# Two attention score products written as full-height matmuls over zero-padded keys, in place of pairs of half-height ones, in a two-layer decoder kernel

## The reference, cut to what matters

```python
# self-attention, 16 heads of 64
q = jnp.einsum('bsm,hmd->bhsd', x, kernel[0])
k = jnp.einsum('bsm,hmd->bhsd', x, kernel[1])
scores = jnp.einsum('bhsd,bhtd->bhst', q, k) * scale
attn = jax.nn.softmax(scores, axis=-1)
out = jnp.einsum('bhst,bhtd->bhsd', attn, v)
...
# cross-attention, 16 heads of 16, keys and values from the context
q = _split_heads(query @ Wq.T + bq)
k = _split_heads(key @ Wk.T + bk)
scores = jnp.einsum('bhnd,bhmd->bhnm', q, k)
attn = jax.nn.softmax(scores, axis=-1)
```

## Time and profile before

| | |
|---|---|
| median of the runs | 1388.13 us |
| the profiled execution, its own time | 1388.13 us |
| its span (first to last instruction) | 1386.4 us |
| mean granted TensorE clock | 0.963 of full |
| busy: TensorE / VectorE / ScalarE / GpSimd | 1161.0 / 750.3 / 732.8 / 380.4 us |
| chain that ended last | TensorE 64%, VectorE 15%, ScalarE 10% |

### The profile page before, as it was taken

How to read it: one execution, slowest core, us unless ns; L and a number is a source line. 1 busy time by engine, 2 the same in 40 slices (tenths; PEclk the granted TensorE clock), 3 DMA queues, 4 the chain that set the end, 5 groups by cost and what they waited for, 6 DMA issues and landing times.

```text
span 1386.4 us, 19831 instructions
## 1 busy us (share of the span) xinstructions
PE 1161.0 (84%) x6458; PEld 770.1 (56%) x6458; DVE 750.3 (54%) x1815; ACT 732.8 (53%) x1866; POOL 380.4 (27%) x881
## 2 busy tenths in 40 slices
PE   6897876999899976799889977699989997779955
PEld 2454544775555644676455554477555564467643
DVE  1563375655464368546545437655545436855644
ACT  1555345575465355557456534556645635555833
POOL 1232301542034310153213430154203332016420
PEclk9998998999999999899999999899999999989978
DMA  9101300000000000000000000000000000000000
GB/s 248 63 1 54 93 1 1 1 1 1 1 0 17 1 23 1 3 0 1 1 1 16 1 23 1 2 1 1 1 1 0 17 1 1 1 1 1 1 0 16
DMA packets 27895, 20.77 MB, mean 15 GB/s; under 512 B 14412, under 2 KB 27148, under 8 KB 27660
## 3 DMA queue, kind: packets, MB, share of 16 engines
q1 hardware_dynamic: 27196, 17.83, 5.0%
q10 hardware_dynamic: 592, 1.59, 0.3%
HBM read 17.32 MB, written 2.10 MB: 14 GB/s over the span
## 4 chain that ended last, share of the span: by engine, by line
PE 64%; DVE 15%; ACT 10%; issue 7%; POOL 3%; DMA 1%; ACTq 0%; SPq 0%; POOLq 0%; DVEq 0%
PE PS L495 8%; PE PS L559 7%; PE PS L841 7%; PE PS L482 5%; PE PS L572 5%; PE PS L547 4%; PE PS L586 4%; PE PS L617 4%; PE PS L602 4%; PE PS L815 3%; PE PS L706 2%; PE PS L692 2%; PE PS L853 2%; ACT work L1316 1%; DVE work L1591 1%
## 5 line engine op out<-in xcount | busy, mean ns | idle before, releaser
L1849 POOL TENSOR_TENSOR rstd<-var,minus_half 128x2 f32<-128x2 f32 x80 | 56.4, 705 | 522.3 <-DVE nmean L1409 522.3
L1138 ACT ACTIVATE work<-PS,nmax 128x256 f32<-128x256 f32 x256 | 117.9, 472 | 99.5 <-DVE nmax L1461 99.5
L1844 POOL TENSOR_TENSOR pool_pause<-minus_half 128x1 f32<-128x1 f32 x96 | 18.6, 194 | 440.3 <-DVE inv L1468 359.0
L1316 ACT ACTIVATE work<-PS,nmax 120x256 f32<-120x256 f32 x256 | 118.4, 483 | 24.7 <-DVE nmax L1726 24.5
L841 PE MATMUL PS<-work 128*120 128x256 f32 x512 | 119.7, 384 | 3.9 <-ACT work L1101 3.9
L1461 DVE TENSOR_REDUCE nmax<-PS 128x2 f32<-128x512 f32 x128 | 82.2, 684 | 68.7 <-PE PS L572 68.2
L1863 POOL TENSOR_SCALAR work<-work,inv 128x256 f32<-128x256 f32 x256 | 118.1, 483 | 0.0
L1726 DVE TENSOR_REDUCE nmax<-PS 120x2 f32<-120x512 f32 x128 | 86.3, 686 | 53.3 <-PE PS L841 48.6
L841 PEld LDWEIGHTS PS<-work 128*120 128x120 f32 x512 | 90.8, 183 | 29.8 <-issue 12.8
L1903 POOL TENSOR_SCALAR work<-work,head_mask 128x120 f32<-128x120 f32 x256 | 107.3, 447 | 0.0
L1109 ACT ACTIVATE x_room<-res,nshift,rstd 128x256 f32<-128x256 f32 x96 | 52.3, 592 | 101.9 <-POOL nshift L1851 101.9
(11 more groups left out here) (258 smaller groups left out, 2439.9 us busy)
## 6 DMA issues: line engine op xcount, KB each, us to landing
xa<-in_x_dram SPq DMA_DIRECT2D x4, 512.0 KB, 3.7
out_dram<-x_room SPq DMA_DIRECT2D x4, 512.0 KB, 3.7
rows<-in_rows_dram ACTq DMA_DIRECT2D x1, 1536.0 KB, 8.5
late<-in_L_attn_W_dram SPq DMA_DIRECT2D x2, 768.0 KB, 7.6
wv<-in_L_attn_kernel_dram SPq DMA_DIRECT2D x2, 512.0 KB, 8.9
wq<-in_L_attn_kernel_dram SPq DMA_DIRECT2D x2, 512.0 KB, 9.5
wk<-in_L_attn_kernel_dram SPq DMA_DIRECT2D x2, 512.0 KB, 7.7
wo<-in_L_attn_WO_dram SPq DMA_DIRECT2D x2, 512.0 KB, 7.7
```

The source lines that it names most:

```text
L1138: op = act.activation(e0[:, u % 2, st, hh, :], bank(2 + hh)[:, st * S:(st + 1) * S], ACT.Exp, bias=nmax0[:, u % 2, hh, st:st + 1], accum_o ...
L1316: op = act.activation(e1[:, par, r, kv, :], bank(4 + n % 4)[0:M, kv * S:(kv + 1) * S], ACT.Exp, bias=nmax1[:, par, r, kv:kv + 1], accum_ou ...
```

## The change

Keys of the self-attention are kept in a tile twice as wide, `k0[P, 2, NB, 2, S]`. It is zeroed once at the start; for each group VectorE copies head 0's 64 partitions into the columns of head 0 and head 1's 64 partitions into the columns of head 1, in two copies, so that each column holds one head's key and zeros for the other head. `scores0` then makes one product with all 128 rows and 512 columns for each query block `st`: two products instead of four. Banks now belong to query blocks, no longer to heads, and the waits between `scores0`, `max0` and `exp0` go by query block. In the cross-attention GpSimd masks 8 copies of the keys for each group instead of 4 (with `head_mask` instead of `quarter_mask`, which goes), and `scores_x` makes its two products of 480 columns with 128 rows instead of 64.

```diff
-        quarter_mask = sb("quarter_mask", [P, HC // 2])
-        k0 = sb("k0", [P, 2, NB, S])
+        k0 = sb("k0", [P, 2, NB, 2, S])
-        kxm = view(work, 6144, P, [2, HC // 2, M])
+        kxm = view(work, 6144, P, [2, HC, M])
...
         def scores0(it, u):
-                if u > 0:
-                    pe.wait_ge(p0_done.sem, p0_done.at(it, 2 * u))
                 for st in range(TS):
-                    for hh in range(2):
-                        rows = slice(hh * DH0, (hh + 1) * DH0)
-                        mm = pe.matmul(bank(2 + hh)[:, st * S:(st + 1) * S],
-                                       q0[rows, j % 2, b * S + st * P:b * S + (st + 1) * P],
-                                       k0[rows, j % 2, b, :], start=True, stop=True)
-                        if st == TS - 1:
-                            mm.then_inc(s0_done.sem, 1)
+                    if u > 0:
+                        pe.wait_ge(p0_done.sem, p0_done.at(it, TS * (u - 1) + st + 1))
+                    pe.matmul(bank(2 + st), q0[:, j % 2, b * S + st * P:b * S + (st + 1) * P],
+                              k0[:, j % 2, b, :, :], start=True, stop=True).then_inc(s0_done.sem, 1)
...
         def scores_x(it, n):
                 for g in range(2):
-                    rows = slice(64 * g, 64 * (g + 1))
-                    mm = pe.matmul(bank(4 + 2 * (n % 2) + g)[:, 0:4 * M], qx[rows, c, b * S + st * P:b * S + (st + 1) * P],
-                                   kxm[rows, n // 2 % 2, :, :], start=True, stop=True)
+                    mm = pe.matmul(bank(4 + 2 * (n % 2) + g)[:, 0:4 * M], qx[:, c, b * S + st * P:b * S + (st + 1) * P],
+                                   kxm[:, n // 2 % 2, 4 * g:4 * g + 4, :], start=True, stop=True)
...
         def exp0(it, u):
-                for hh in range(2):
-                    act.wait_ge(m0_done.sem, m0_done.at(it, 2 * u + hh + 1))
+                for st in range(TS):
+                    act.wait_ge(m0_done.sem, m0_done.at(it, TS * u + st + 1))
...
-                    for st in range(TS):
-                        op = act.activation(e0[:, u % 2, st, hh, :], bank(2 + hh)[:, st * S:(st + 1) * S], ACT.Exp,
+                    for hh in range(2):
+                        op = act.activation(e0[:, u % 2, st, hh, :], bank(2 + st)[:, hh * S:(hh + 1) * S], ACT.Exp,
...
         def keep_k0(it, j):
-                dve.tensor_copy(k0[:, j % 2, :, :].rearrange("p b s -> p (b s)"), bank(1)).then_inc(k0_kept.sem, 1)
+                for hh in range(2):
+                    rows = slice(hh * DH0, (hh + 1) * DH0)
+                    op = dve.tensor_copy(k0[rows, j % 2, :, hh, :], bank(1)[rows, :].rearrange("p (b s) -> p b s", b=NB))
+                op.then_inc(k0_kept.sem, 1)
...
+            dve.memset(k0[:, :, :, :, :], 0.0)
             dve.memset(vxp[:, :, :, :, :], 0.0)
...
                 def mask_x(m):
-                    for h in range(HC // 2):
+                    for h in range(HC):
                         op = pool.tensor_scalar(kxm[:, m % 2, h, :], kx[:, c, b * M:(b + 1) * M],
-                                                quarter_mask[:, h:h + 1], 1.0, ALU.mult, ALU.mult)
+                                                head_mask[:, h:h + 1], 1.0, ALU.mult, ALU.mult)
```

More of the change, by code:

```diff
@@ L183, in decoder @@
         q0 = view(work, 12288, P, [2, N])
-        k0 = sb("k0", [P, 2, NB, S])
+        k0 = sb("k0", [P, 2, NB, 2, S])
         e0 = view(work, 4096, P, [2, TS, 2, S])
         e0t = view(work, 6144, P, [2, 2, TS, S])
-        nmax0 = sb("nmax0", [P, 2, 2, TS])
-        sum0 = sb("sum0", [P, 2, 2, TS])
-        inv0 = sb("inv0", [P, 2, 2, TS])
+        nmax0 = sb("nmax0", [P, 2, TS, 2])
+        sum0 = sb("sum0", [P, 2, TS, 2])
+        inv0 = sb("inv0", [P, 2, TS, 2])
         o0t = view(work, 8192, P, [J, N])
@@ L324, in decoder @@
         U0 = J * NB
-        s0_done, m0_done, p0_done = signal("s0_done", U0 * 2), signal("m0_done", U0 * 2), signal("p0_done", U0 * 2)
+        s0_done, m0_done, p0_done = signal("s0_done", U0 * TS), signal("m0_done", U0 * TS), signal("p0_done", U0 * TS)
         i0_done, n0_done = signal("i0_done", U0), signal("n0_done", U0)
@@ L392, in decoder @@
         gsum_done, gg2_wide, base_done = signal_rounds("gg_dve_steps", ("sum", "layer 2 in columns", "base"))
-        N_CONST = 12
+        N_CONST = 11
         N_ZEROED = 1
@@ L1132, in exp0 @@
             def exp0(it, u):
-                for hh in range(2):
-                    act.wait_ge(m0_done.sem, m0_done.at(it, 2 * u + hh + 1))
+                for st in range(TS):
+                    act.wait_ge(m0_done.sem, m0_done.at(it, TS * u + st + 1))
                     if u > 1:
                         act.wait_ge(t0_done.sem, t0_done.at(it, 2 * (u - 1)))
-                    for st in range(TS):
-                        op = act.activation(e0[:, u % 2, st, hh, :], bank(2 + hh)[:, st * S:(st + 1) * S], ACT.Exp,
-                                            bias=nmax0[:, u % 2, hh, st:st + 1], accum_out=sum0[:, u % 2, hh, st:st + 1])
+                    for hh in range(2):
+                        op = act.activation(e0[:, u % 2, st, hh, :], bank(2 + st)[:, hh * S:(hh + 1) * S], ACT.Exp,
+                                            bias=nmax0[:, u % 2, st, hh:hh + 1], accum_out=sum0[:, u % 2, st, hh:hh + 1])
                     op.then_inc(p0_done.sem, 1)
@@ L1455, in keep_k0 @@
                 dve.wait_ge(k0_done.sem, k0_done.at(it, j + 1))
-                dve.tensor_copy(k0[:, j % 2, :, :].rearrange("p b s -> p (b s)"), bank(1)).then_inc(k0_kept.sem, 1)
+                for hh in range(2):
+                    rows = slice(hh * DH0, (hh + 1) * DH0)
+                    op = dve.tensor_copy(k0[rows, j % 2, :, hh, :], bank(1)[rows, :].rearrange("p (b s) -> p b s", b=NB))
+                op.then_inc(k0_kept.sem, 1)
             def max0(it, u):
-                for hh in range(2):
-                    dve.wait_ge(s0_done.sem, s0_done.at(it, 2 * u + hh + 1))
-                    dve.tensor_reduce(nmax0[:, u % 2, hh, :], bank(2 + hh).rearrange("p (t s) -> p t s", t=TS), AX.X, ALU.max,
+                for st in range(TS):
+                    dve.wait_ge(s0_done.sem, s0_done.at(it, TS * u + st + 1))
+                    dve.tensor_reduce(nmax0[:, u % 2, st, :], bank(2 + st).rearrange("p (h s) -> p h s", h=2), AX.X, ALU.max,
                                       negate=True).then_inc(m0_done.sem, 1)
             def inverse0(it, u):
-                dve.wait_ge(p0_done.sem, p0_done.at(it, 2 * (u + 1)))
+                dve.wait_ge(p0_done.sem, p0_done.at(it, TS * (u + 1)))
                 if u > 1:
@@ L1863, in layer0 @@
                             op = pool.tensor_scalar(e0[:, u % 2, st, hh, :], e0[:, u % 2, st, hh, :],
-                                                    inv0[:, u % 2, hh, st:st + 1], 1.0, ALU.mult, ALU.mult)
+                                                    inv0[:, u % 2, st, hh:hh + 1], 1.0, ALU.mult, ALU.mult)
                     op.then_inc(n0_done.sem, 1)
```

3 lines of the change are left out of this document (removed).

## The result

The changed kernel takes 1428.27 us in the median of four runs (1427.72 to 1434.54), the kernel before 1388.43 (1387.81 to 1392.27). The ratio is 1.0291, with a 95% interval of 1.0257 to 1.0325: slower by 2.9%. The forecast was 1429.2 us. The profiled execution has a span of 1427.4 us against 1386.4.

What follows compares the result with a forecast made beforehand. The prediction took TensorE to bound the self-attention and only some scores to be waited for in the cross-attention. Terms of 24.2, 3.0, 4.1 and 9.8 us sum to 41.1 on 1388.1: 1429.2 us, 3.0% slower, range 1416 to 1441.

Steps and rivals of the forecast that it cites:

- What bounds the kernel: Self-attention, second pass: the chain is nearly all TensorE, 5.00 us a unit, so work added there adds to the time.
- The pairing: Self-attention scores: half-height products run two by two in 0.213 us slots; full height loses this, +0.55 us a unit.
- Term A: Self-attention units in which TensorE leads: 44 units at +0.55 us each, 24.2 us.
- Term B: First two self-attention steps and key copies: 0.6 us in passes two to four, 1.16 in the first, 3.0 us.
- Term C: Last two self-attention steps: scores 15 +0.8 us three times, +1.7 in the first pass at low clock, 4.1 us.
- Term D: Cross-attention scores: +0.61 us a step, exposed at steps 0, 1, 4 and 6 of each pass, 9.8 us in four.
- What was said to cost nothing: GpSimd's eight masks, zeroing the wide key tile, and maxima, exponentials and inverses: hidden or as many as before.
- Rival 1: Mode gaps don't come back: 0.85 us a unit, 1442 us; with all cross steps exposed too, 1452; chance 10%.
- Rival 2: Slack swallows more: cross-attention hides all but two steps, first and last self-attention steps cost nothing; 1417 us, chance 15%.
- Rival 3: Full-height weight loads are exposed, 0.19 us an instruction, 0.76 a unit, about 33 us more: 1463 us; chance 2%.
- Rival 4: Not slower: splitting the wait for four exponentials gives back 0.9 us a unit, 1372 us at all 64; chance 3%.

Runs made afterwards that it cites:

- self_only: Changed kernel with the cross-attention scores and four masks of the kernel before, so the self-attention part alone; 1422.91 us, ratio 1.0226 to the kernel before.
- cross_only: Kernel before with the changed `scores_x` and `mask_x`, so the cross-attention part alone; 1403.93 us, ratio 1.0089 to the kernel before.
- unpaired: Kernel before with both heads' self-attention score products on rows 0 to 63, so no two run beside each other; 1448.11 us, ratio 1.0421.
- weigh_first_split: Kernel before with weighing moved ahead of the projection and keys copied sequence by sequence, a signal for each; 1382.30 us, ratio 0.9949.
- one_wait: Changed kernel with each unit's self-attention scores waiting once for all four exponentials instead of twice for two; 1433.25 us.
- one_key_copy: Changed kernel without the second of the two copies of each group's keys (head 1's keys stay zero); 1428.88 us.
- masks4: Changed kernel with GpSimd making four of the eight key masks of each cross-attention step group; 1435.20 us.
- weigh_first: Kernel before with TensorE's weighing of unit u - 2 moved ahead of the projection in each step; 1394.62 us, ratio 1.0027.
- unpaired_x: Kernel before with both products of each cross-attention score step on rows 0 to 63, so they can't run beside each other; 1418.84 us.

## Why the prediction was right

The time, 1429.2 against 1428.27 us, hides errors of both signs. By its own steps:

**What bounds the kernel.** Right. The stage was TensorE's before and after, and each part's cost arrived there (`self_only`, `cross_only`).

**The pairing.** Right: slots of 0.216 us, two products in each, and 0.43 us an instruction of 512 columns without them. `unpaired` shows it apart from zeros and height. One reading was too narrow: such gaps lie not only behind half-height products. Ahead of the column-wise weighing the projection's last product takes 0.52 us instead of 0.43, too, in both kernels, and leaving out one change of arrangement gave 0.14 us (`weigh_first_split`).

**Term A, +0.55 us a unit, 24.2 us.** Mis-sized. A unit grew by 0.46. I had taken 0.21 us as what leaving the half-height arrangement costs, and counted the projection as unchanged at 1.91; its first product was 0.10 us slower for it too. From scores 2 to scores 14 each of the later passes grew by 5.6 us, against 6.6 forecast, and the first by 3.8 against 4.4: some 20.6 us in all (what I expected of `self_only` has 5.75 and 3.9 for the two, which is a little too much).

**Term B, the first two steps, 3.0 us.** Mis-sized: 0.96 us in each of the later passes, and 1.45 in the first with its first keys, in sum 4.3. The split wait gave back 0.86 us here (`one_wait`), as forecast. The key copy took 0.5 us at step 2 of the later passes, the upper end of the forecast, and 0.7 at step 2 of the first pass, for 0.47, besides the 0.7 for the first keys (`one_key_copy`).

**Term C, the last two steps, 4.1 us.** Mis-sized, 1.5 us measured. In the later passes step 14 is 0.12 us shorter from start to start (3.76 us for 3.88) and scores 15 cost 0.74, near the 0.8 forecast: 0.63 a pass. In the first pass the +1.7 us did not come; from scores 14 to the cross-attention it took 0.37 us less than before. TensorE's timeline of the changed kernel there answers to the earlier trace rows:

```profile
135.16 3.44 PE L569 MATMUL PS<-k,work 128*128 128x512 f32 x4
138.53 1.08 PE L596 MATMUL PS<-work 128*64 128x256 f32 x8
139.55 2.86 PE L611 MATMUL PS<-wo,work 128*128 128x256 f32 x12
```

The scores did take 3.4 us at the low clock. But the weighing behind them took 1.08 us where it had taken 1.98: the clock rose at their end instead of later, and gave back what they cost. I had priced the instruction at the low clock and left the clock's own course as it was. That it turned out so well is chance. In `one_wait` and `masks4` the same scores took 3.73 us and the weighing behind them 1.70 and 1.69, still at the low clock, and the stretch was 1.0 us longer than before, not shorter.

**Term D, cross-attention, 9.8 us.** Mis-sized the other way: 11.7. Three of the four places where scores are waited for were the right ones. From scores to scores, in every pass, steps 0, 1 and 4 grew by 0.60, 0.56 and 0.57 us. But step 6 grew by 0.07 only: its transposes had waited 0.42 us for ScalarE, and the longer scores took that time. Steps 2, 3 and 5, taken as free, grew by 0.13, 0.09 and 0.23. The fourth place was the last step, 7: its transposes come 0.69 us later behind the scores (2.77 for 2.08), and the rest of the stage was 0.43 to 1.13 us longer. The timeline of all engines, second pass, answers to the earlier trace rows:

```profile
522.70 1.88 PE L676 MATMUL PS<-work 128*128 128x480 f32 x4
524.41 1.04 PE L685 MATMUL PS<-ident,work 128*120 128x128 f32 x8
524.61 1.16 DVE L1557 TENSOR_REDUCE maxx<-PS 128x8 f32<-128x960 f32 x1 [2.80 <-PE PS L676]
532.85 1.16 DVE L1557 TENSOR_REDUCE maxx<-PS 128x8 f32<-128x960 f32 x1 [1.51 <-PE PS L676]
```

From scores to transposes it is 1.71 us at step 4, not 1.62, so 0.70 where nothing hides it, and not 0.61. I had taken the pace from a row in the middle of full-height work (L638); behind a wait or column-wise products the first instruction takes 0.51 us, not 0.40.

**What was said to cost nothing** did: masks (`masks4`); the zeroing, since the first projections start at 29.49 to 30.38 us in the changed kernel and at 29.98 before; and the exponentials, with ScalarE busy for 733.8 us and 732.8 before.

**Outside the two stages** nothing was forecast, and 2.5 us were found. 1.2 of them lie behind the first pass, where the granted clock was 0.94 and not 0.96; for the rest no cause is shown, but two kernels whose code is the same there differ by up to 3 us. A, B, C and D as measured give 20.6 + 4.3 + 1.5 + 11.7 = 38.1 us, against 41.1 forecast; a later start of 0.4 us and the 2.5 made it 41.0. So the mechanism was right, and that the total came within 1 us is luck: A and C were 6.2 us too high, B and D 3.2 too low, and the wander was 2.9.

**The rivals.** Rival 1's missing gaps did come back, 0.40 us of them a unit. Rival 2's slack was there at step 6 of the cross-attention and at the last steps of the first pass, but not in the sum. Rival 3 falls with `unpaired`. Rival 4 is bounded by `one_wait`: the split is worth 1.0 us a pass.

## What to carry to other kernels

Two products of half the rows, on different halves of the array, cost the time of one; padding them with zeros to one of full height doubles the columns that are streamed, and saves only the change of arrangement, here 0.40 us against 0.85. Where TensorE leads, first count columns a slot, then count how often a step changes between row pairs, column pairs and full height, and order the calls so that it does so less often; then look for the copy that has become late. Read a change of this size from stage lengths between fixed instructions, which in the TensorE-bound stage of passes two to four mostly repeat within 0.04 us, not from medians that wander by 5 us; and where one of them doesn't repeat, look at the granted clock of its stretch first.

## What the runs showed of the hardware that was not expected

- A stage led by TensorE repeats within 0.04 us between passes two to four and between runs (116.02 to 116.06 in the changed kernel's two runs, `self_only` and `masks4`), with one exception, the 109.76 us of one pass of `weigh_first` beside 108.10 in the others, where the mean granted clock was 0.72 over 6 us. Why it fell there is open: TensorE had idled 1.99 us before these scores, and 1.98 us at the same place of the second pass, where the clock stayed at 1.00. Stages with idle TensorE come in two or more lengths: the cross-attention of before at 40.1 or 41.0 us, the last part at 193.6 to 194.4 with a granted clock of 0.90 or at 196.8 to 198.0 with 0.86 to 0.88.
- The granted clock stayed at half for 10.00 us in which TensorE was never idle, in half-height products that ran one at a time and transposes (`unpaired_x`), and the stage was longer so in three passes of four.
- Where the clock rises again moves from run to run by more than a microsecond: behind the scores of step 15 in the first pass the same weighing took 1.08 us in the changed kernel and 1.70 in `one_wait`.
- Each change between full and half height costs 0.19 to 0.20 us, half of it ahead of the first product of the new arrangement and half behind it.
